# A sort's scatters held two block steps later behind TensorE in a graph network kernel

## The chip, the cores and the metric

One core of a Trainium2 chip runs the whole program in one launch. The metric is the device time of that core in microseconds, the median of several runs. The kernel before took 1187.74 us (three runs: 1185.68, 1187.74, 1198.05).

## The reference, cut to what matters

The input is a table `x` of 50,000 nodes by 128 features and 12,500 edges, each with a source node, a destination node and 40 attributes (3, 5 and 32 of them). With `h = relu(layernorm(x))` the result is `x` plus a graph layer of `h`:

```
h  = maximum(layernorm(x), 0)
xx = resmlp(h, weights 0)                 # every node: x + silu(silu(x) w1 + b1) w2 + b2, then silu, wout
xs, xp, xd = resmlp(h, weights 1..3)[dst] # gathered for each edge
s = xx + segment_sum(gs * xs, src)        # gs, gp, gd come from the 32 edge attributes
p = segment_sum(gp * xp, src);  d = segment_sum(gd * xd, src)   # gp also times pij (3), gd times dij (5)
y = s + (pa * pb).sum + (da * db).sum     # pa, pb = halves of p w_pp;  da, db = halves of d w_pd
out = x + resmlp(y, weights 4)
```

The segment sums need the edges ordered by source node, and the kernel sorts them itself.

## The kernel before, in words

**Stages.** The program has three stages: a node stage (about the first 410 us), an edge stage and a final stage. In the node stage the 50,000 rows are cut into 98 blocks of 512 rows (four tiles of 128). Each block is loaded, normalised (VectorE and ScalarE share it, lines 618 to 637 and 774 to 788), stored to a table `node_h`, transposed by TensorE (L871), sent through three matrix products (L884, L891, L899) with a ScalarE activation after each of the first three TensorE operations (L798, L808, L817), copied out (L823) and stored. TensorE does this for 94 blocks in a software pipeline: in step k it transposes block k, does the first product of block k-1, the second of block k-2 and the output product of block k-3. One such step is called a block step here, and its number is that of the block transposed.

**The sort beside it.** In the same stage a radix sort with two passes, one per digit of the source number, orders 98 tiles of 128 edges. For each pass VectorE makes one-hot rows of the digits (L664), TensorE counts them (L834), and VectorE makes starting ranks (L672, L674). Then, in 14 chunks of seven tiles, TensorE keeps running counts (L859) and VectorE picks each edge's rank out of them (L681) and writes the ranks of the chunk (L693). GpSimd then moves the edges: each tile is one indirect DMA that writes 128 rows of 42 words to a table in device memory (L506). The first pass writes to `edges_by_low`, which GpSimd loads back into SBUF (L544, three parts) when all 98 scatters have landed; the second pass starts from that (digits L648, one-hots L664, in step 49 of VectorE's program), and writes to `edges_by_src`.

**Order around the change.** Each engine's program is written out by hand. VectorE's and ScalarE's work for a block is tied to TensorE by counting semaphores; `chunk()` (L268) places chunk c of a pass in step `chunks + 5c//2`. The ranks of a chunk after the first are written one step later. The first pass has `chunks` = 5, the second 53. GpSimd has nothing of the block work, only the scatters. `scatter` (L501) waits for the ranks of its chunk, and before each of its seven tiles it calls `keep_pace` (L474), which waits for TensorE:

```
quarter = 4 * ps.scatters + 5 * t // 3
n = quarter // 4
```

The quarter modulo four says which event is waited for: transposes of block n-1, first product of block n-2, second product of block n-3, or output product of block n-4. All four events lie in TensorE's step n-1. So twelve scatters are let go in five block steps, and the wait before tile 97 is for step 44 in the first pass and step 92 in the second. The field `scatters` is read in `keep_pace` only.

**What follows the scatters.** After the first pass GpSimd waits for all scatters and issues the three loads of `pay`; VectorE's next instruction (L648) waits for the first of them, and TensorE counts the new one-hots at fixed places of steps 49 to 52. Blocks 50 to 55 are normalised by ScalarE alone. After the second pass SyncE, which has issued the block loads and stores before, waits for all scatters and loads the first edge groups (`load_group`, L57 to L68); GpSimd waits for the first of these before it gathers rows (L74), and TensorE's first work of the edge stage (L1760) waits for the gathers.

Of the kernel before, what the change touches and what calls it, by code (L numbers as in the profile page):

```python
# [78 lines left out]
def gnn_kernel(nc, x, src, dst, attr3, attr32, attr5, w_rs, w_rp, w_rd, w_pp, w_pd,  # L79
# [54 lines left out]
    with ctx:  # L134
# [125 lines left out]
        class Pass:  # L260


            def __init__(self, n, made_at, counted_at, seeded_at, based_at, picked_at, chunks, alone, dram, width):
                self.n, self.made_at, self.counted_at, self.seeded_at = n, made_at, counted_at, seeded_at
                self.based_at, self.picked_at = based_at, picked_at
                self.chunks, self.scatters, self.alone, self.dram, self.width = chunks, chunks, alone, dram, width

            def chunk(self, k, lag=0):  # L268

# [1748 lines left out]
```

## Time and profile before

| what | value |
|---|---|
| median of three runs | 1187.74 us |
| the profiled execution | 1187.62 us, span 1185.8 us |
| TensorE busy | 1088.6 us, 92% |
| VectorE busy | 688.9 us, 58% |
| ScalarE busy | 736.6 us, 62% |
| GpSimd busy | 471.7 us, 40% |
| scatters of the first pass | 98, from 46.2 to 208.8 us |
| scatters of the second pass | 98, from 247.9 to 400.5 us |

Times in rows are from the start of the span. Outside the span lie 1.8 us of the profiled execution. In a timeline row the first number is the start and the second the duration, `x` the number of instructions merged, and the bracket gives the idle time of the engine before it and what ended it. The name "remote" or "another core or an unknown queue" stands where the releaser is not known to the profile.

### The profile page before, as it was taken

The page shows a single profiled execution, that of the slowest core. Times are in us where ns is not written, and L with a number is a line of the kernel's source. Part 1 is how long each engine was busy: PE and PEld are TensorE (multiplying, and loading weights), DVE is VectorE, ACT ScalarE, POOL GpSimd, SP SyncE. Part 2 cuts the span into 40 slices and gives each one's busy share as a digit, 9 for nine tenths or more (in the row PEclk, how much of TensorE's full clock was granted, in tenths as well). Part 3 has the DMA queues.
Part 4 walks back from the last instruction along what each step waited for, and adds up shares of the span by engine and source line. Part 5 has one row for each costly group of instructions (what it writes and reads, how often), then busy time and mean ns, then how long its engine had stood idle before and what let it go on. Part 6 is the DMA issues. An engine that isn't in the chain of part 4 may idle for free.

```text
span 1185.8 us, 22908 instructions
## 1 busy us (share of the span) xinstructions
PE 1088.6 (92%) x6267; PEld 711.7 (60%) x6267; DVE 688.9 (58%) x2413; ACT 736.6 (62%) x1379; POOL 471.7 (40%) x433
## 2 busy tenths in 40 slices
PE   4978998987898659999999999999979999999998
PEld 2645665765666326666666666666736666666665
DVE  8976776766666226656665665655633444444432
ACT  4656878966778635665565565555536666666664
POOL 2355666155666442556556656655440000000000
PEclk9988999999999879999999999999999999999999
DMA  9667767855674443665556555555549999999984
GB/s 267 208 201 232 225 223 222 296 170 175 224 228 155 142 94 75 115 118 107 97 102 107 99 95 106 101 96 92 101 69 240 282 268 274 274 271 273 269 275 142
DMA packets 319187, 210.81 MB, mean 178 GB/s; under 512 B 204084, under 2 KB 240830, under 8 KB 318963
## 3 DMA queue, kind: packets, MB, share of 16 engines
q1 hardware_dynamic: 280770, 164.67, 50.7%
q0 software_dynamic: 24208, 19.29, 10.3%
q10 hardware_dynamic: 14112, 25.70, 6.2%
q8 instruction: 44, 0.72, 0.3%
q14 instruction: 53, 0.43, 0.1%
HBM read 107.15 MB, written 102.42 MB: 177 GB/s over the span
## 4 chain that ended last, share of the span: by engine, by line
PE 83%; DVE 6%; issue 5%; ACT 2%; another core or an unknown queue 2%; DMA 2%; POOL 0%; SPq 0%; ACTq 0%; POOLq 0%; DVEq 0%
PE quad L1133 8%; PE bank L1147 7%; PE bank L1769 6%; PE quad L884 5%; PE quad L1139 5%; PE bank L1779 5%; PE bank L899 5%; PE bank L1845 4%; PE quad L891 4%; PE bank L1815 4%; PE bank L1846 3%; PE quad L871 3%; PE quad L1855 2%; PE quad L1122 2%
## 5 line engine op out<-in xcount | busy, mean ns | idle before, releaser
L1421 POOL DMA_INDIRECT node_sums<-rowout,row_i x98 | 154.8, 1580 | 49.6 <-issue 28.7
L74 POOL DMA_INDIRECT yin<-node_h,er x98 | 99.2, 1012 | 165.1 <-DMA nxt<-edges_by_src 130.9
L1054 DVE TENSOR_TENSOR rowout<-bank,xin 128x512 f32<-128x512 f32 x98 | 67.8, 692 | 142.7 <-PE bank L1147 141.7
L1147 PEld LDWEIGHTS bank<-wo_sb,s 128*128 128x128 f32 x784 | 102.8, 191 | 47.8 <-issue 47.8
L899 PEld LDWEIGHTS bank<-wo_sb,s 128*128 128x128 f32 x720 | 95.3, 194 | 54.6 <-issue 54.5
L506 POOL DMA_INDIRECT edges_by_low<-pay,rank_i x98 | 99.7, 1017 | 69.5 <-issue 28.9
L1473 DVE SCALAR_TENSOR_TENSOR h<-bank,b_sb,hT 128x512 f32<-128x512 f32 (+1 forms) x75 | 55.5, 740 | 123.3 <-PE bank L1779 113.6
L506 POOL DMA_INDIRECT edges_by_src<-pay,rank_i x98 | 98.9, 1009 | 60.8 <-issue 24.4
L784 ACT ACTIVATE xn<-xin,nbias,rnorm 128x128 f32<-128x128 f32 x222 | 106.4, 493 | 13.0 <-DVE nbias L616 10.5
L681 DVE SCALAR_TENSOR_TENSOR picked<-bank,onehot 128x256 bf16<-128x256 f32 (+1 forms) x196 | 67.5, 387 | 74.1 <-PE bank L859 29.6
L1133 PE MATMUL quad<-s,w_sb 128*128 128x512 f32 x196 | 103.8, 612 | 0.8 <-ACT s L1071 0.7
L1147 PE MATMUL bank<-wo_sb,s 128*128 128x128 f32 x784 | 103.5, 275 | 0.9 <-DVE rowout L1054 0.9
L899 PE MATMUL bank<-wo_sb,s 128*128 128x128 f32 x720 | 96.9, 278 | 7.9 <-ACT rowout L823 5.7
L884 PE MATMUL quad<-s,w_sb 128*128 128x512 f32 x188 | 101.8, 625 | 0.1
L565 DVE BATCH_NORM_STATS2 stat<-xin 128x6 f32<-128x128 f32 x392 | 98.6, 283 | 1.1 <-DMA xin<-in_x_dram 1.1
L1652 ACT ACTIVATE s<-h 128x512 f32<-128x512 f32 (+1 forms) x75 | 46.6, 622 | 72.7 <-DVE h L1473 56.6
L1681 ACT COPY AB<-bank 128x512 f32<-128x512 f32 x98 | 58.1, 593 | 54.1 <-PE bank L1846 41.9
L1769 PE MATMUL bank<-s,w_sb 128*128 128x512 f32 (+1 forms) x150 | 79.9, 615 | 6.9 <-ACT s L1644 4.8
L871 PE MATMUL quad<-ident,xn 128*128 128x128 f32 x284 | 45.5, 284 | 38.7 <-issue 21.0
L808 ACT ACTIVATE s<-quad,b_sb 128x512 f32<-128x512 f32 x94 | 64.6, 687 | 21.4 <-PE quad L884 11.9
L1779 PE MATMUL bank<-s,w_sb 128*128 128x512 f32 (+1 forms) x150 | 76.2, 590 | 0.1
L891 PE MATMUL quad<-s,w_sb 128*128 128x512 f32 x142 | 75.7, 616 | 0.0
(208 smaller groups left out, 2254.4 us busy)
## 6 DMA issues: line engine op xcount, KB each, us to landing
xin<-in_x_dram SPq DMA_DIRECT2D x196, 256.0 KB
node_h<-xn SPq DMA_DIRECT2D x98, 256.0 KB
out_dram<-rowout ACTq DMA_DIRECT2D x98, 256.0 KB
node_sums<-rowout SPq DMA_DIRECT2D x90, 256.0 KB
yin<-node_sums SPq DMA_DIRECT2D x53, 256.0 KB, 3.7
yin<-node_sums SPq DMA_DIRECT2D x180, 64.0 KB, 3.2
src_in_every_row<-edge_src_row SPq DMA_DIRECT2D x24, 256.0 KB
border_sums_by_tile<-border_sums SPq DMA_DIRECT2D x24, 256.0 KB, 2.1
```

Of the source, the lines that this page charges most:

```text
L74: pool.indirect_dma_start(out=xg[:, s, j, :], out_offset=None, in_=x, in_offset=bass.IndirectOffsetOnAxis(ap=er[:, s, j, 1:2].bitcast(mybi ...
L506: nc.gpsimd.indirect_dma_start(out=ps.dram, out_offset=bass.IndirectOffsetOnAxis(ap=rank_i[:, t:t + 1], axis=0), in_=pay[:, t, :], in_offs ...
L565: last = nc.vector.bn_stats(stat[:, b % 32, j, :], xin[:, s, j, :])
L784: ins = nc.scalar.activation(xn[:, b % 4, j, :], xin[:, s, j, :], ACT.Relu, bias=nbias[:, q, i:i + 1], scale=rnorm[:, q, i:i + 1])
L884: nc.tensor.matmul(BANK_A[:, :], w1_sb[:, m, :], s1[:, (k - 1) % 3, :], start=True, stop=True).then_inc(a_done, 1)
L891: nc.tensor.matmul(BANK_X[(k - 2) % 4][:, :], w2_sb[:, m, :], s2[:, (k - 2) % 3, :], start=False, stop=True, skip_group_check=True).then_i ...
L899: last = nc.tensor.matmul(BANK_O[:, j * P:(j + 1) * P], s3[:, (k - 3) % 3, j * P:(j + 1) * P], wo_sb[:, m, :], start=True, stop=True)
L1133: nc.tensor.matmul(BANK_A[:, :], w1_sb[:, m, :], s1[:, s, :], start=True, stop=True).then_inc(a_done, 1)
L1147: last = nc.tensor.matmul(BANK_O[:, j * P:(j + 1) * P], s3[:, s, j * P:(j + 1) * P], wo_sb[:, m, :], start=True, stop=True)
L1421: nc.gpsimd.indirect_dma_start(out=ysum, out_offset=bass.IndirectOffsetOnAxis(ap=row_i[:, t % 2, j:j + 1], axis=0), in_=urow[:, t % 2, j, ...
L1769: nc.tensor.matmul(BANK_A[:, 0:e], w1_sb[:, MLP[m], :], s1[:, k % 2, 0:e], start=True, stop=True).then_inc(a_done, 1)
L1779: nc.tensor.matmul(BANK_B[:, 0:e], w2_sb[:, MLP[m], :], s2[:, m, 0:e], start=True, stop=True).then_inc(b_done, 1)
```

## The change

Both passes get `scatters = chunks + 2` in place of `scatters = chunks`: 7 and 55 in place of 5 and 53. The quarter number of every scatter grows by eight, so that each of the 196 waits is for the same kind of event two block steps later. Tile 97 waits for step 46 in the first pass and for step 94 in the second (where the counts are capped at 94 and 90). No instruction is added or taken away.

```diff
@@ -263,7 +263,7 @@
             def __init__(self, n, made_at, counted_at, seeded_at, based_at, picked_at, chunks, alone, dram, width):
                 self.n, self.made_at, self.counted_at, self.seeded_at = n, made_at, counted_at, seeded_at
                 self.based_at, self.picked_at = based_at, picked_at
-                self.chunks, self.scatters, self.alone, self.dram, self.width = chunks, chunks, alone, dram, width
+                self.chunks, self.scatters, self.alone, self.dram, self.width = chunks, chunks + 2, alone, dram, width
 
             def chunk(self, k, lag=0):
```

## Rows read from the trace of the kernel before

**Rows 1.** The page, costliest groups: the scatters of the first pass.
```profile
L506 POOL DMA_INDIRECT edges_by_low<-pay,rank_i x98 | 99.7, 1017 | 69.5 <-issue 28.9
```

**Rows 2.** Windows, transposes L871 alone: stretch, length, PE, PEld, clock, DMA share, GB/s.
```profile
44.45:115.62 71.17, 9.70 (x56) 6.96 (x57) 0.86 0.69 223
115.62:205.50 89.88, 14.76 (x96) 10.55 (x97) 1.00 0.71 221
208.91:221.66 12.75, 2.46 (x16) 1.86 (x17) 1.00 0.89 307
260.61:301.80 41.19, 6.00 (x37) 4.28 (x37) 0.96 0.60 192
301.80:398.36 96.56, 16.07 (x104) 11.34 (x105) 1.00 0.59 195
```

**Rows 3.** Timeline of GpSimd, first and last scatter of one chunk.
```profile
58.91 0.96 POOL L506 DMA_INDIRECT edges_by_low<-pay,rank_i  x1 [3.96 <-DVE rank_i L693]
...
66.67 0.96 POOL L506 DMA_INDIRECT edges_by_low<-pay,rank_i  x1 [0.31 <-issue]
```

**Rows 4.** Timelines of TensorE and ScalarE beside that chunk, steps 10 and 11.
```profile
62.45 0.60 PE L871 MATMUL quad<-ident,xn 128*128 128x128 f32 x4
...
70.77 1.87 PE L884 MATMUL quad<-s,w_sb 128*128 128x512 f32 x2
...
67.59 0.60 ACT L798 ACTIVATE s<-quad 128x512 f32<-128x512 f32 x1 [3.73 <-remote]
```

**Rows 5.** The same timelines in the second pass, steps 61 and 91, and a scatter.
```profile
276.65 0.60 PE L871 MATMUL quad<-ident,xn 128*128 128x128 f32 x4
...
280.42 0.60 ACT L798 ACTIVATE s<-quad 128x512 f32<-128x512 f32 x1 [1.66 <-remote]
...
393.92 0.60 PE L871 MATMUL bank<-ident,xn 128*128 128x128 f32 x4
...
396.33 0.60 ACT L798 ACTIVATE s<-bank 128x512 f32<-128x512 f32 x1 [1.63 <-PE quad L884]
...
396.57 1.07 POOL L506 DMA_INDIRECT edges_by_src<-pay,rank_i  x1 [1.25 <-remote]
```

**Rows 6.** Timelines where the first pass ends: TensorE, GpSimd, VectorE, ScalarE.
```profile
205.97 1.02 PE L884 MATMUL quad<-s,w_sb 128*128 128x512 f32 x2
...
212.96 1.02 PE L884 MATMUL quad<-s,w_sb 128*128 128x512 f32 x2
...
239.82 2.52 PE L834 MATMUL bank<-onehot,ident_h 128*128 128x196 bf16 x28
...
208.77 1.14 POOL L506 DMA_INDIRECT edges_by_low<-pay,rank_i  x1 [0.30 <-issue]
212.12 1.67 POOL L544 DMA_DIRECT2D pay<-edges_by_low  x3 [2.21 <-DMA edges_by_low<-pay,rank_i]
...
217.88 0.18 DVE L648 CAST digit_i<-pay 128x28 int32<-128x28 f32 x1 [4.89 <-DMA pay<-edges_by_low]
...
229.94 7.66 DVE L664 TENSOR_SCALAR onehot<-digits_h,digit_f 128x196 bf16<-128x196 bf16 x42
...
242.45 0.36 DVE L749 CAST counts_h<-bank 128x196 bf16<-128x196 f32 x1 [2.52 <-PE bank L834]
...
252.29 0.49 ACT L784 ACTIVATE xn<-xin,nbias,rnorm 128x128 f32<-128x128 f32 x1 [1.34 <-DVE nbias L616]
```

**Rows 7.** Timelines where the second pass ends: GpSimd, TensorE, SyncE's queue.
```profile
400.53 1.16 POOL L506 DMA_INDIRECT edges_by_src<-pay,rank_i  x1 [0.30 <-issue]
412.97 0.99 POOL L74 DMA_INDIRECT yin<-node_h,er  x1 [11.27 <-DMA er<-edges_by_src]
...
401.44 0.60 PE L871 MATMUL quad<-ident,xn 128*128 128x128 f32 x4
...
403.82 1.10 PE L884 MATMUL quad<-s,w_sb 128*128 128x512 f32 x2
...
419.56 1.08 PE L1760 MATMUL quad<-ident,yin 128*128 128x128 f32 x4 [12.73 <-DMA yin<-node_h,er]
...
410.08 0.37 SPq L64 DMA_DIRECT2D er<-edges_by_src  x1
```

## The prediction

> **What bounds the kernel now.** The change moves 196 waits of one engine, so I read in this order: what the moved instruction costs, how fast the node stage goes with and without it, what happens in single steps, and then the two places where other work waits for the last scatter. The page's costliest groups show that a scatter takes 1017 ns of GpSimd [rows 1]. That engine is not the bound. TensorE's block step is, and the windows over the transposes give its length, as four transposes are one step [rows 2]. There are 14 steps in 71.17 us (5.08 us each) while the first pass's scatters start, then 24 steps in 89.88 us (3.745 us each). With no scatter running, the windows' third row has four steps in 12.75 us (3.19 us each). In the second pass there are 9 steps in 41.19 us (4.58 us each) and then 26 in 96.56 us (3.714 us each). So the stage is slow early in either pass, and fastest where GpSimd rests. DMA is no busier in the slow stretch than in the fast one, 0.69 and 0.71 [rows 2].
>
> The timelines say what differs. Early on, the scatters wait for ranks and not for TensorE. When a chunk's ranks come, all seven of its scatters go out back to back, and the row that opens such a run names the ranks as the releaser [rows 3]. The old pace allows it, because the wait before tile 7 is for an output product of step 6, while its ranks are written in VectorE's iteration 8. The gates move 7 x 5/12 = 2.92 steps per chunk and the ranks 2.5, so the ranks' lateness shrinks by 0.42 a chunk and is gone after about five. In those runs ScalarE gets its transposed block late. In step 10 the transposes start at 62.45 and ScalarE's activation of them at 67.59, which is 5.14 us later and just as the run of seven is over [rows 3, 4]. In step 61 it is 3.77 us. In a stretch where TensorE paces the scatters the long delay is 2.41 us, and the delay without trouble is under 1 us [rows 5]. I count six delays of the long kind, all beside runs of at least six scatters: three of 5.1 to 5.9 us in the first pass, three of 3.7 to 3.8 us in the second (a seventh, of 3.7 us, stands in a later, paced stretch). What holds the transposes' signal back is not in the trace, as the releaser is "remote". That it goes with unbroken runs is my reading.
>
> **The change part by part.** No instruction is added, and no other queue gains or loses a DMA. GpSimd's queue holds, behind the scatters, the three loads back, the corrections and the first gathers.
>
> *The pace early in each pass.* With eight quarters more, tile 7 waits for step 8 and tile 14 for step 11, about when their ranks are there. Ranks then no longer release seven at once, and each scatter has its own gate, 5/12 of a step apart: 1.56 us at 3.745 us a step, against 1.29 us from start to start inside a run (66.67 - 58.91 over six) [rows 2, 3]. I cost this as a gain. If the six long delays shrink to the paced 2.41 us, it is 3 x (5.14 - 2.41) + 3 x (3.77 - 2.41) = 8.2 + 4.1 = 12.3 us [rows 4, 5]. The ends are 0, if the delay comes from something else, and 26.5 us, if both slow stretches run at the later pace: 71.17 - 14 x 3.745 = 18.7 and 41.19 - 9 x 3.714 = 7.8 [rows 2]. The upper end has the clock in it too. Behind the long delay a pair of products takes 1.87 us in place of 1.02 [rows 4, 6], and the granted clock of that stretch is 0.86, between the two levels of 1.2 and 2.4 GHz [rows 2]. I take 12.3 because it rests on delays that I can point at.
>
> *The end of the first pass.* The last gate moves from the first product of step 44 to that of step 46, 212.96 - 205.97 = 6.99 us later [rows 6]. The last scatter, the load back and VectorE's first digit follow it, since each waits for the one before: 208.77, 212.12 and 217.88 become about 215.8, 219.1 and 224.9. VectorE already waited 4.89 us for this load, so all of the 6.99 us reaches the one-hots [rows 6]. TensorE has some air. Its last 28 counts start at 239.82 and take 2.52 us, so the last seven start near 241.7, and the last one-hot ends at 229.94 + 7.66 = 237.60. That is 4 us of air, so TensorE itself waits 3 us. VectorE has less. Behind the one-hots it does statistics, waits 2.52 us for the counts, and then makes ranks and norm constants for which ScalarE waits 1.34 us. That chain moves by 6.99 - 2.52 = 4.5 us and the next blocks with it [rows 6]. Ends: 3.0 and 7.0 us. I take 4.5, as ScalarE is seen waiting on this chain.
>
> *Two more steps with scatters.* Steps 45 and 46 ran with none, from 208.91, at 3.19 us on average; at the paced 3.745 us they cost 2 x 0.55 = 1.1 us [rows 2]. Steps 5 and 6, and 53, lose a few in turn, which I leave at nothing. Ends: 0 and 2 us.
>
> *The end of the second pass.* SyncE issues the first load of the edge stage at 410.08, long after the last scatter's start at 400.53, so it was waiting for its own stores and not for the scatters [rows 7]. The cover is thin. A scatter has landed about 2.21 us after its end [rows 6], so the old slack is 410.08 - (400.53 + 1.16 + 2.21) = 6.2 us. The new group of four starts at most 2.65 us behind the last transposes at 401.44 (396.57 - 393.92) and its last 3.96 us after its first, so at 408.05, and at the earliest at 404.92, when the product of step 94 is through. It lands between 408.3 and 411.4 [rows 5 to 7]. The load then moves by 0 to 1.3 us, and everything behind it (the gathers, TensorE's idle 12.73 us) moves with it. I take 0.7 us.
>
> *Sum.* -12.3 + 4.5 + 1.1 + 0.7 = -6.0 us. The profiled execution of before took 1187.62 us and the median is 1187.74, so either base gives 1181.6 us.
>
> **A rule against the gain.** The slow stretch moved 223 GB/s and the fast one 221, so traffic does not tell the two apart, and a run of scatters brings only a few more small writes into a step [rows 2]. The Trainium skill, "DMA: Bandwidth & Descriptors", section "Issuing engines are not separate DMA queues", says that DMAs of all issuing engines end on the same 16 DMA engines and interleave there. By that rule alone what counts is the work, which is unchanged, and the gain is nothing.
>
> **The rivals.**
> 1. *The runs were not the cause.* The same writes on the same engines cost the same wherever they stand, and only the late end is paid: 1187.6 + 4.5 + 1.1 + 0.7 = 1193.9 us. For it: "remote" names no engine, and delays of 2.41 us go on in paced stretches. Against it: the steps without scatters are the fastest of all [rows 2, 5].
> 2. *The whole early slowness was the runs.* The gain is 26.5 us, and 1187.6 - 26.5 + 6.3 = 1167.4 us. For it: paced steps reach 3.7 us right behind the slow ones. Against it: in the first slow stretch weights and zeros are moved too, and VectorE is still busy after the one-hots.
> 3. *Slower: the load back lands in a crowd.* It starts near 219.1, in a stretch with DMA at 0.89 and 307 GB/s [rows 2], and now shares it with the last scatters' writes. Every microsecond beyond the 6.99 goes into VectorE's wait. Before, it took 217.88 - 212.12 = 5.76 us. If it takes twice that and the gain fails too, the time is 1187.6 + (6.99 + 5.76 - 2.52) + 1.8 = 1199.6 us. It decides against the kernel once the load back lasts over 11 us. Before, it began in that same stretch and was not slow, which speaks against it.
> 4. *The waits don't bind.* If ranks were late throughout, nothing would move: 1187.7 us. The rows against it are those in which TensorE releases scatters to the end.
>
> **How the numbers follow.** The forecast gets 0.50, rival 1 gets 0.20, rival 2 gets 0.15, rival 3 gets 0.08 and rival 4 gets 0.07. The forecast's own range, with a gain of 6 to 18 us and costs of 4 to 9, is 1174 to 1191 us. To hold 8 in 10 the whole range reaches up to rival 1 with its upper costs, 1197, and down near rival 2, 1170. About 1% (11.9 us) is what a measurement of this kernel can tell from no change. Faster by over 1% is rival 2 and a fifth of the forecast: 0.15 + 0.09 = 0.24. Slower by over 1% is rival 3 and a little of rival 1: 0.09. Within 1%: 0.67.
>
> **What would show it.** In the new trace the scatters of chunks 1 to 4 should have gaps of TensorE's making, and the releases by ranks should be almost gone. No activation L798 should start over 3 us behind its transposes before step 20. The 14 steps from the seventh on should take some 60 to 65 us. The first digit (L648) should come about 7 us later against step 49's transposes, and VectorE's wait of 2.52 us for the counts should vanish. The first load of the edge stage should be within 1.5 us of its old distance from the last transposes. I am wrong if delays of 5 us stay although the runs are broken, if new runs of seven form under the new gates, or if the load back takes over 8 us.

## The result, and the profile after

The changed kernel takes 1171.02 us (median of four runs, 1169.22 to 1175.29). Beside it the kernel before took 1186.71 us (four runs, 1184.07 to 1198.05). The medians differ by 15.7 us, or 1.3%. The recorded ratio, which is not that of the medians, is 0.9853 with a 95% interval of 0.9816 to 0.989. So the kernel is faster here by 1.3 to 1.5%. The forecast was 1181.6 us, a gain of 6.0 us. Its sign was right and its size was not. On three other chips the same change makes the kernel 0.4 to 0.5% slower, as the experiments show, so the sign held only for a chip like this one. I call the chip of these two kernels the first chip. The record has no number for it and does not say outright that it is one and the same for both.

The profiled execution of after took 1172.58 us with a span of 1168.8 us, against 1185.8 us before. I laid the two spans side by side, cut at TensorE's transposes. These are windows over all engines of after: stretch, length, then busy time and count for PE, PEld, DVE, ACT and POOL, then the granted clock, DMA share and GB/s.

```profile
44.45:100.27 55.82, 50.12 (x261) 33.62 (x260) 51.33 (x300) 42.26 (x85) 33.40 (x33) 0.97 0.85 269
100.27:189.18 88.91, 82.19 (x442) 55.87 (x441) 66.64 (x358) 72.54 (x145) 58.94 (x58) 1.00 0.72 230
189.18:207.32 18.14, 15.85 (x82) 10.43 (x81) 4.56 (x21) 14.93 (x31) 9.22 (x11) 1.00 0.71 222
207.32:235.23 27.91, 24.76 (x184) 18.81 (x183) 25.04 (x132) 19.55 (x41) 3.28 (x4) 1.00 0.62 230
235.23:246.20 10.97, 10.20 (x58) 6.93 (x56) 10.63 (x64) 9.42 (x20) 6.47 (x7) 1.00 0.64 206
246.20:281.87 35.67, 31.52 (x174) 21.01 (x173) 25.19 (x140) 26.97 (x55) 21.33 (x23) 1.00 0.66 213
281.87:378.31 96.44, 87.84 (x472) 59.29 (x473) 61.13 (x328) 77.62 (x156) 61.41 (x62) 1.00 0.60 197
```

The same windows of before, for the stretches that changed most (the first, fourth, fifth and sixth):

```profile
44.45:115.62 71.17, 56.84 (x261) 37.33 (x260) 51.41 (x300) 43.44 (x85) 38.20 (x38) 0.86 0.69 223
...
221.66:246.02 24.36, 24.27 (x185) 18.93 (x184) 21.49 (x113) 19.19 (x41) 3.15 (x4) 1.00 0.63 230
246.02:260.61 14.59, 10.56 (x58) 6.85 (x56) 13.45 (x78) 9.57 (x21) 8.65 (x9) 1.00 0.49 157
260.61:301.80 41.19, 32.92 (x173) 22.07 (x173) 21.94 (x125) 27.31 (x55) 24.94 (x25) 0.96 0.60 192
```

The counts of matmuls agree, so each pair of windows holds the same work. A window's length less its PE busy time is TensorE's idle time, and that splits every difference into waiting and slower work:

| block steps | before | after | difference | of it TensorE idle | of it TensorE busy |
|---|---|---|---|---|---|
| 6 to 20 | 71.17 | 55.82 | -15.35 | -8.63 | -6.72 |
| 20 to 44 | 89.88 | 88.91 | -0.97 | -0.81 | -0.16 |
| 44 to 49 | 16.16 | 18.14 | +1.98 | +1.77 | +0.21 |
| 49 to 54, first pass's end | 24.36 | 27.91 | +3.55 | +3.06 | +0.49 |
| 54 to 57 | 14.59 | 10.97 | -3.62 | -3.26 | -0.36 |
| 57 to 66 | 41.19 | 35.67 | -5.52 | -4.12 | -1.40 |
| 66 to 92 | 96.56 | 96.44 | -0.12 | | |
| 92 to 93 | 3.08 | 3.38 | +0.30 | | |
| step 93 to the first edge load | 8.64 | 10.00 | +1.36 | | |
| the rest of the span | 775.7 | 777.1 | +1.4 | | |

That is -17.0 us in all. The gain is 25.5 us in four rows of the table and the losses are 8.6 us.

**The runs are broken up.** In the timeline of GpSimd in after, the scatters that answer to [rows 3] go out in threes, and TensorE opens each group. Not every later run is that short: the longest has eight scatters, from 148.5 to 159.5 us. In before the first of seven had waited for its ranks.

```profile
58.81 0.96 POOL L506 DMA_INDIRECT edges_by_low<-pay,rank_i  x1 [1.07 <-PE bank L899]
60.07 1.05 POOL L506 DMA_INDIRECT edges_by_low<-pay,rank_i  x1 [0.30 <-issue]
61.43 1.15 POOL L506 DMA_INDIRECT edges_by_low<-pay,rank_i  x1 [0.31 <-issue]
63.51 0.96 POOL L506 DMA_INDIRECT edges_by_low<-pay,rank_i  x1 [0.93 <-PE bank L899]
```

**The longest delays before step 20 are gone.** For [rows 4], step 10, the timelines of TensorE and ScalarE give the transposes at 61.67 and ScalarE's activation of them 2.08 us later (5.14 before). The longest such delay before step 20 is in step 17, 2.96 us:

```profile
61.67 0.63 PE L871 MATMUL quad<-ident,xn 128*128 128x128 f32 x4
...
87.59 0.60 PE L871 MATMUL quad<-ident,xn 128*128 128x128 f32 x4
...
63.75 0.60 ACT L798 ACTIVATE s<-quad 128x512 f32<-128x512 f32 x1
...
90.55 0.60 ACT L798 ACTIVATE s<-quad 128x512 f32<-128x512 f32 x1
```

The three longest of steps 6 to 19 were 5.14, 5.88 and 5.11 us and are 2.96, 2.59 and 2.58 us, which is 8.0 us less. TensorE's idle time there fell by 8.6 us. Its products also run at the higher level of the clock again: the granted clock of the stretch rose from 0.86 to 0.97 and PE busy fell by 6.7 us for the same 261 matmuls. Further on, two delays over 3 us remain, of 3.02 us in step 37 and 3.22 us in step 61.

**Other signals than the transposes' are late too.** In before, the timelines of TensorE and ScalarE show it twice. Near 84 us ScalarE waits 4.92 us for an output product that ended at 79.05, and TensorE then waits 3.78 us for ScalarE's copy of it. Near 256 us ScalarE starts on a second product (L891) and an output product (L899) 4.1 and 4.8 us after their ends, at 252.44 and 253.33:

```profile
84.47 0.58 ACT L823 COPY rowout<-bank 128x512 f32<-128x512 f32 x1 [4.92 <-remote]
85.20 1.19 PE L899 MATMUL bank<-wo_sb,s 128*128 128x128 f32 x4 [3.78 <-ACT rowout L823]
...
251.42 1.02 PE L891 MATMUL quad<-s,w_sb 128*128 128x512 f32 x2
252.28 1.05 PE L899 MATMUL bank<-wo_sb,s 128*128 128x128 f32 x8
...
256.54 0.69 ACT L817 ACTIVATE s<-quad,b_sb 128x512 f32<-128x512 f32 x1 [1.79 <-remote]
258.09 0.59 ACT L823 COPY rowout<-bank 128x512 f32<-128x512 f32 x1 [0.86 <-remote]
```

The trace also records when semaphores were raised, though no view prints it and some records are missing. Here each raise from 44 us to the last transposes that belongs to one instruction without doubt (about three quarters of TensorE's) is set against that instruction's end. The ends of matmuls are modelled.

| signals of | before: recorded | over 1 us late | latest | after: recorded | over 1 us late | latest |
|---|---|---|---|---|---|---|
| TensorE | 284 | 78 | 5.40 us | 293 | 65 | 2.73 us |
| VectorE | 392 | 1 | 1.31 us | 373 | 0 | 1.00 us |
| ScalarE | 222 | 0 | 0.01 us | 206 | 0 | 0.01 us |

The late ones belong to every kind of TensorE's work, and they arrive in bursts. In before L859, L884 and L891 end at 63.82, 64.68 and 65.54, and their signals are recorded at 69.07, 69.11 and 69.15. In steps 57 to 66 of before 11 recorded signals are over 1.8 us late, and two of them are of transposes; in after 3 are, and one of them is. The mean lateness of TensorE's signals fell from 1.24 to 0.53 us in steps 6 to 20 and from 1.38 to 0.58 us in steps 57 to 66. In steps 20 to 44, where the time hardly changed, it went from 0.54 to 0.63 us.

**The first pass's end is paid for.** The timelines of after answer to [rows 6], in the order of GpSimd, VectorE and TensorE:

```profile
200.67 0.96 POOL L506 DMA_INDIRECT edges_by_low<-pay,rank_i  x1 [0.30 <-issue]
204.00 1.67 POOL L544 DMA_DIRECT2D pay<-edges_by_low  x3 [2.37 <-DMA edges_by_low<-pay,rank_i]
...
209.73 0.18 DVE L648 CAST digit_i<-pay 128x28 int32<-128x28 f32 x1 [11.77 <-DMA pay<-edges_by_low]
...
231.69 0.34 DVE L749 CAST counts_h<-bank 128x196 bf16<-128x196 f32 x1
...
207.32 0.60 PE L871 MATMUL quad<-ident,xn 128*128 128x128 f32 x4
211.79 0.76 PE L834 MATMUL bank<-onehot,ident_h 128*128 128x196 bf16 x7 [1.25 <-DVE onehot L664]
...
229.49 0.76 PE L834 MATMUL bank<-onehot,ident_h 128*128 128x196 bf16 x7 [0.50 <-DVE onehot L664]
...
232.09 0.26 PE L840 MATMUL bank<-counts_h,ones_h 128*128 128x196 bf16 x1 [1.40 <-DVE counts_h L749]
```

L648 stood 3.78 us ahead of step 49's transposes before (217.88 and 221.66) and stands 2.41 us behind them now, 6.2 us later. VectorE's wait of 2.52 us for the counts has vanished, and TensorE waits 1.25 + 0.50 + 1.40 = 3.15 us instead. The load back took 209.73 - 204.00 = 5.73 us, against 5.76 before.

**The second pass's end**, for [rows 7], from the timelines of GpSimd, SyncE's queue and TensorE:

```profile
388.47 0.96 POOL L506 DMA_INDIRECT edges_by_src<-pay,rank_i  x1 [0.30 <-issue]
394.60 0.99 POOL L74 DMA_INDIRECT yin<-node_h,er  x1 [5.17 <-DMA er<-edges_by_src]
...
385.62 5.78 SPq L410 DMA_DIRECT2D node_h<-xn  x4
391.69 0.37 SPq L64 DMA_DIRECT2D er<-edges_by_src  x1
...
401.20 1.09 PE L1760 MATMUL quad<-ident,yin 128*128 128x128 f32 x4 [12.85 <-DMA yin<-node_h,er]
```

GpSimd waits 5.17 us for the edge load in place of 11.27. SyncE issues that load 0.29 us after its last node store has been issued (385.62 + 5.78), and 2.26 us after the last scatter's end, about the 2.21 us in which a scatter landed in [rows 6]. Both are near enough to be the one that bound it. Against step 93's transposes the last scatter starts 7.7 us later than before (from 0.9 us ahead of them to 6.8 us behind), and the load goes out 1.4 us later. So 6.3 us of the shift were hidden.

### The profile page after: what moved, and what is told of

Its sections match the earlier page's. It is cut to its first block, busy times and chain, and to the rows that moved or that the text cites. A ratio compares the mean times of both kernels' runs of the same rounds, so it can differ in the third digit from the quotient of the medians.

```text
span 1168.8 us, 22908 instructions
## 1 busy us (share of the span) xinstructions
PE 1082.8 (93%) x6267; PEld 707.0 (60%) x6267; DVE 689.3 (59%) x2413; ACT 736.0 (63%) x1379; POOL 468.9 (40%) x433
## 4 chain that ended last, share of the span: by engine, by line
PE 81%; DVE 6%; issue 6%; ACT 2%; DMA 2%; another core or an unknown queue 1%; POOL 1%; SPq 0%; ACTq 0%; POOLq 0%; DVEq 0%
PE quad L1133 8%; PE bank L1147 8%; PE bank L1769 6%; PE quad L1139 5%; PE bank L1779 5%; PE quad L884 5%; PE bank L899 5%; PE bank L1845 4%; PE bank L1815 4%; PE quad L891 4%; PE bank L1846 4%; PE quad L871 2%; PE quad L1122 2%; PE quad L1854 2%; PE quad L1855 2%
## 5 line engine op out<-in xcount | busy, mean ns | idle before, releaser
L899 PEld LDWEIGHTS bank<-wo_sb,s 128*128 128x128 f32 x720 | 93.3, 191 | 50.6 <-issue 49.9
L784 ACT ACTIVATE xn<-xin,nbias,rnorm 128x128 f32<-128x128 f32 x222 | 106.5, 493 | 12.4 <-DVE nbias L616 10.5
L1133 PE MATMUL quad<-s,w_sb 128*128 128x512 f32 x196 | 103.7, 611 | 0.8 <-ACT s L1071 0.7
L899 PE MATMUL bank<-wo_sb,s 128*128 128x128 f32 x720 | 95.9, 276 | 4.3 <-ACT rowout L823 2.3
L884 PE MATMUL quad<-s,w_sb 128*128 128x512 f32 x188 | 98.2, 604 | 1.3 <-ACT s L808 1.3
L1139 PE MATMUL quad<-s,w_sb 128*128 128x512 f32 x148 | 75.6, 592 | 0.0
L808 ACT ACTIVATE s<-quad,b_sb 128x512 f32<-128x512 f32 x94 | 64.6, 687 | 15.1 <-PE quad L884 13.3
L1079 ACT ACTIVATE s<-quad,b_sb 128x512 f32<-128x512 f32 x98 | 66.5, 679 | 11.2 <-PE quad L1133 11.1
```

The lines of the kernel that those rows point to most:

```text
L784: ins = nc.scalar.activation(xn[:, b % 4, j, :], xin[:, s, j, :], ACT.Relu, bias=nbias[:, q, i:i + 1], scale=rnorm[:, q, i:i + 1])
L884: nc.tensor.matmul(BANK_A[:, :], w1_sb[:, m, :], s1[:, (k - 1) % 3, :], start=True, stop=True).then_inc(a_done, 1)
L899: last = nc.tensor.matmul(BANK_O[:, j * P:(j + 1) * P], s3[:, (k - 3) % 3, j * P:(j + 1) * P], wo_sb[:, m, :], start=True, stop=True)
L1133: nc.tensor.matmul(BANK_A[:, :], w1_sb[:, m, :], s1[:, s, :], start=True, stop=True).then_inc(a_done, 1)
L1139: nc.tensor.matmul(BANK_X[s][:, :], w2_sb[:, m, :], s2[:, s, :], start=in_squares(k, 2), stop=True, skip_group_check=True).then_inc(b_done, 1)
```

## The experiments

Two theories stood against each other.

- **A.** The change gains because it takes away the late signals from TensorE to ScalarE, and costs what the ends cost.
- **B.** The unbroken runs of scatters do the harm by themselves, wherever the kernel runs, or the later scatters gain in some other way.

The four sets of experiments ran on four other chips (numbered 2, 10, 11 and 9 in the record), and there the kernel before takes 1116 to 1117 us, 70 us less than on the first. I compare every kernel only with the kernel before on its own chip.

### Set 1: each pass alone, a stretched pace, and gaps

First pass alone:

```diff
-self.scatters = chunks
+self.scatters = chunks + (2 if n == 0 else 0)
```

> Only the first pass is moved by two steps. Theory (unbroken runs of six or more scatters hold back TensorE's signals; broken by the later gates they don't): steps 6 to 20 take 56 us as after the change, in place of 71.2; the first pass's end costs some 5 us; the second pass keeps its long delays of 3.7 us. About 1187 - 15.3 - 1 + 2 + 3.5 = 1176 us. Rival (the gain comes from where the two trains stand to each other or to the other work of the whole stage, not from runs): no such split, with steps 6 to 20 over 65 us or a sum of the two halves far from 16 us.

Second pass alone, `chunks + (2 if n == 1 else 0)`:

> Only the second pass is moved. Theory: steps 6 to 20 take 71 us as before, the first pass ends as before, steps 54 to 66 lose about 9 us, the end of the stage costs 1.4 us: about 1187 - 9 + 1.4 = 1179 us. Rival (whole stage): no gain without the first pass's shift, 1187 us.

Both passes start two steps later and end at the old steps:

```diff
-self.scatters = chunks
+self.scatters = chunks + 2
...
-quarter = 4 * ps.scatters + 5 * t // 3
+quarter = 4 * ps.scatters + 153 * t // 97
```

> Gates start two steps later as in the change, but run closer together (153 quarters over 97 tiles), so that the last gate of either pass is where it was before, steps 44 and 92. Theory: the runs are broken all the same, so the gain of about 25 us stays (15.3 + 1 + 3.6 + 5.5), and the costs of the late ends (5.5 at the first, 1.4 at the second) go: 1162 to 1166 us. Rival (the whole train must stand two steps later): half the gain at most, 1175 to 1182 us.

Gaps on GpSimd in the kernel before, a memset of 1.3 us behind the third and sixth scatter of the first five chunks of either pass:

```diff
+if t < 35 and t % 7 in (2, 5):
+    if pads[0]:
+        pool.wait_ge(s_pad, pads[0])
+    pads[0] += 1
+    nc.gpsimd.memset(st32[:, REST:T, :], 0.0).then_inc(s_pad, 1)
```

> Gates as before the change; in chunks 0 to 4 of either pass a 1.27 us memset stands on GpSimd behind the third and the sixth scatter of the seven, so no run is longer than three. Theory: delays over 3 us behind the transposes go, steps 6 to 20 take 56 to 60 us, neither pass ends later: 1164 to 1172 us. Rival (the position of the scatters in the steps, by the gates, makes the gain): 1186 to 1190 us. Second rival (any busy GpSimd delays the others): no gain either.

Measured against 1116.92 us (22 runs) for the kernel before:

| kernel | median, us | ratio, 95% |
|---|---|---|
| first pass alone | 1121.62 | 1.0039 (1.0022 to 1.0056) |
| second pass alone | 1116.41 | 1.0007 (0.9994 to 1.002) |
| start later, end the same | 1115.92 | 0.999 (0.9981 to 1.0) |
| gaps | 1130.4 | 1.0117 (1.01 to 1.0134) |

None gained. The times expected for this set were those of a chip with late signals, and so none of them could be tried. The change's price stood alone: 4.7 us of the first pass and nothing of the second. The gaps made the kernel slower. They delay GpSimd's train, and most of their price lies where other work waits for it: against the kernel before of sets 2 and 4, steps 6 to 20 take 2.9 us more (51.92), steps 49 to 54 take 5.8 us more and the rest from step 93 on 5.3 us more, with the edge load 15.4 us behind step 93's transposes in place of 8.6. This experiment can't speak on the late signals, because here there are none, as the next set shows.

### Set 2: before and after, unaltered

> The kernel before, unchanged, profiled beside the next one. If this chip delays the transposes' signal as in the first trace, steps 6 to 20 take some 71 us and the kernel 1187 us. If not (as in the four runs so far, where the kernel before took 1117 us), steps 6 to 20 take about 51 us, GpSimd issues over 80 scatters back to back in each pass with no activation L798 more than 1.2 us behind its transposes, and the kernel takes 1117 us.

> The changed kernel, timed against the kernel before on one chip. If the chip shows the delays: some 16 us faster. If it does not: theory 1 (the gain was only the shortened delays, and what is left is the cost of the late end of the first pass) gives 4.5 to 5 us slower, about 1122 us. Theory 2 (a gain that needs no delays) gives faster by 10 us or more on this chip too.

Before took 1116.15 us (10 runs) and after 1120.21 us (7 runs), a ratio of 1.0042 (1.0029 to 1.0056). So the change itself is 4 us slower here. It was timed on two more chips in sets 3 and 4. Set 4 gave the trace that I read closest. First its windows over all engines, of the kernel before, for steps 6 to 20 and 57 to 66:

```profile
44.42:93.48 49.06, 46.70 (x262) 32.73 (x260) 48.47 (x287) 42.62 (x85) 34.63 (x35) 1.00 0.92 307
223.26:253.14 29.88, 29.88 (x175) 21.23 (x174) 24.74 (x137) 27.56 (x55) 22.43 (x23) 1.00 0.84 262
```

The first stretch takes 49.06 us where the first chip took 71.17, with the same matmuls and 2.36 us of idle time in place of 14.33. Then the timelines of TensorE, ScalarE and GpSimd for step 10 and its chunk of scatters, which answer to [rows 3, 4]:

```profile
59.95 0.60 PE L871 MATMUL quad<-ident,xn 128*128 128x128 f32 x4
...
60.64 0.60 ACT L798 ACTIVATE s<-quad 128x512 f32<-128x512 f32 x1
...
57.33 0.95 POOL L506 DMA_INDIRECT edges_by_low<-pay,rank_i  x1 [2.18 <-DVE rank_i L693]
58.59 1.14 POOL L506 DMA_INDIRECT edges_by_low<-pay,rank_i  x1 [0.31 <-PE quad L884]
60.03 0.96 POOL L506 DMA_INDIRECT edges_by_low<-pay,rank_i  x1 [0.31 <-issue]
```

The run of seven is there, opened by its ranks as on the first chip, and the activation starts 0.69 us after the transposes begin. From 67.2 to 154.3 us 67 scatters go out without a gap, and in the second pass 91 do, from 224.0 to 343.3. Over all 94 steps the longest delay is 1.15 us (1.13 and less outside step 1). So unbroken runs of scatters don't delay ScalarE by themselves. With the change slower on each of the three chips that ran it, the later scatters don't gain in some other way there either, and theory B falls.

### Set 3: a third chip, and four steps

> The changed kernel once more, unaltered, for a chip on which TensorE's signals come late. Theory A (the gain is the going of the late signals, the price is the first pass's end): where the kernel before takes 1184 to 1190 us, 1170 us, and steps 6 to 20 in 55 to 57 us; where it takes 1116 us, 1120 us. Theory B (the change gains by itself, whatever the signals): under 1 of the kernel before on every chip.

> The first pass alone two steps closer. Theory A: where the kernel before takes 1184 to 1190 us, it keeps the gain of steps 6 to 44 (some 16 us) and pays the first pass's end (some 5 us), and doesn't have the second pass's 9 us: 1176 us. Where the kernel before takes 1116 us: 1121 us, all 4.7 us in steps 49 to 54. Theory B: as the changed kernel's ratio, 0.985, on either.

> Both passes' scatters start two steps later and end at the steps of the kernel before (a pace of 153/97 quarter steps a scatter instead of 5/3). Theory A: where signals come late, the gain of the changed kernel without its price at the first pass's end, 1171 less 4 to 5 = 1166 us, if breaking up the early runs is what counts; where they do not, 1116 us as before. Theory B (the distance at the end matters too): no better than the changed kernel.

With `chunks + 4` in both passes:

> Four steps instead of two, both passes. Theory A: the first pass's end costs by the gate, 3.05 us a step: two steps cost 4.7 us of 6.1, so four cost 4.7 + 6.1 = 10.8 us in steps 49 to 54; at the second pass's end two steps cost nothing that showed, and two more at most their 6.1 us. Where the kernel before takes 1116 us: 1127 to 1133 us. Where it takes 1187 us: 1175 to 1184 us. Theory B (the price is the end's own fixed chain, paid once): 1120 to 1122 us where the kernel before takes 1116.

Measured against 1116.54 us (20 runs):

| kernel | median, us | ratio, 95% |
|---|---|---|
| the change | 1121.41 | 1.0035 (1.002 to 1.005) |
| first pass alone | 1120.75 | 1.0037 (1.0024 to 1.0051) |
| start later, end the same | 1116.39 | 0.9994 (0.9984 to 1.0005) |
| four steps | 1132.23 | 1.0132 (1.0115 to 1.0149) |

The price grows with the steps and lies in two places. These are the windows of steps 49 to 54 over all engines, for the kernel before (set 4), then the first pass alone and then four steps (both set 3):

```profile
187.94:212.30 24.36, 24.27 (x185) 18.93 (x184) 24.00 (x127) 19.20 (x41) 3.29 (x4) 1.00 0.66 242
```

```profile
188.21:217.98 29.77, 26.11 (x184) 19.62 (x183) 25.03 (x132) 19.69 (x41) 3.28 (x4) 0.94 0.60 211
```

```profile
187.94:224.31 36.37, 27.27 (x184) 20.67 (x183) 25.15 (x132) 19.59 (x41) 5.89 (x9) 0.86 0.51 176
```

Two steps cost 5.4 us in this trace and four cost 12.0, a little over two more block steps of 3.05 us for the second two. The timeline of TensorE with four steps shows the wait at the first one-hots:

```profile
200.17 1.32 PE L834 MATMUL bank<-onehot,ident_h 128*128 128x196 bf16 x7 [9.02 <-DVE onehot L664]
```

After an idle time of 9.02 us the same seven counts take 1.32 us in place of 0.76, so the wait costs once more in the clock (0.86 in this stretch). Theory A's 10.8 us left out this part. At the second pass's end, two steps cost nothing that shows, and four push the edge load from 8.6 to 14.0 us behind step 93's transposes. The timelines of GpSimd and SyncE's queue with four steps name the reason:

```profile
363.98 0.96 POOL L506 DMA_INDIRECT edges_by_src<-pay,rank_i  x1 [0.31 <-issue]
...
366.31 0.37 SPq L64 DMA_DIRECT2D er<-edges_by_src  x1
```

The load now goes out 1.37 us after the last scatter has ended. That end is bound by the scatters. With two steps the load keeps its place (8.7 us behind the transposes in all three traces).

### Set 4: a fourth chip, and more small writes

> The changed kernel unaltered on whichever chip this is. Theory A (the gain is the going of late signals; the price is the first pass's end): 4 to 5 us over the kernel before where that takes 1116 us, 14 to 18 us under it where it takes 1184 to 1190 us. Theory B (the change gains by itself): under the kernel before in both.

> The kernel before, unaltered, for its trace on this chip. Theory A: if it takes 1116 us, no transposes wait over 1.2 us for ScalarE and steps 6 to 20 take 49 to 51 us; if it takes 1184 to 1190 us, delays of 2.4 to 5 us beside unbroken runs of scatters, and 65 to 71 us.

One candidate for the late signals was left that I could make here: many small writes beside the scatters.

```diff
+if 7 <= k < 21:
+    for i in (2 * k - 14, 2 * k - 13):
+        sp.dma_start(spare_rows[i * P:(i + 1) * P, :], zeros[:, 0:64]).then_inc(s_spare, 16)
```

In the kernel before:

> The kernel before with two more writes of 128 rows of 256 bytes from a zeroed tile to DRAM in each of SP's block turns 7 to 20 (28 writes, about as many small packets again as the scatters make there). Theory A (many small writes are what makes TensorE's signals late): transposes wait 2 us and more for ScalarE in steps 7 to 20, and these steps take 55 us or more. Theory B (not the packets, but something that this chip does not have): these delays stay under 1.2 us, steps 6 to 20 take 49 to 54 us, and the time is 0 to 5 us over the kernel before.

In the changed kernel:

> The changed kernel with the same 28 small writes. Theory A: less is lost to late signals than without the change, so it is level with or under the run without it. Theory B: the same 4 us over the run without the change as without the writes.

Measured against 1116.71 us (13 runs): the change 1122.96 us, ratio 1.0049 (1.0032 to 1.0066). Before with the writes took 1116.92 us, 1.0005 (0.9993 to 1.0018), and after with the writes 1121.61 us, 1.0046 (1.0029 to 1.0063). With the writes, step 6 to 20 of the kernel before read as follows in the windows of the transposes (length, PE, PEld, clock, DMA share, GB/s):

```profile
44.77:93.81 49.04, 8.45 (x56) 6.54 (x57) 1.00 0.92 278
```

That is 49.04 us against 49.06 without them, and between steps 7 and 20 no activation starts over 0.69 us behind its transposes. So more small packets alone bring no delays on this chip. What they would do on the first chip is not tested, and these writes went out from SyncE's queue, not from GpSimd's. For the changed kernel the expectation was a choice between no loss and the same 4 us. It took 1121.61 us with the writes and 1122.96 without, and the runs of the two overlap, so the writes cost nothing that shows. The change costs 4.7 us with them and 6.3 without.

### The traces in one table

Lengths in us, from transposes to transposes, and from step 93 to the end of the span. The first two rows are the first chip.

| kernel | 6 to 20 | 20 to 49 | 49 to 54 | 54 to 93 | 93 to end |
|---|---|---|---|---|---|
| before, first chip | 71.17 | 106.04 | 24.36 | 155.42 | 784.4 |
| after, first chip | 55.82 | 107.05 | 27.91 | 146.46 | 787.1 |
| before, sets 2 and 4 | 49.05, 49.06 | 94.46, 94.46 | 24.44, 24.36 | 128.02, 128.01 | 772.5, 772.6 |
| after, sets 2, 3, 4 | 49.04, 50.72, 50.73 | 94.47 in each | 28.80, 28.62, 27.54 | 128.07, 128.07, 128.08 | 771.4, 773.3, 774.6 |
| first pass alone, sets 1, 3 | 50.58, 49.04 | 94.46, 94.47 | 29.03, 29.77 | 128.01, 128.02 | 773.0, 772.7 |
| second pass alone | 50.72 | 94.47 | 24.35 | 128.07 | 771.4 |
| start later, end the same | 49.04, 49.05 | 94.47, 94.46 | 24.35, 24.35 | 128.02, 128.02 | 774.4, 773.5 |
| four steps | 49.04 | 94.47 | 36.37 | 128.00 | 777.9 |
| gaps | 51.92 | 94.72 | 30.16 | 128.02 | 777.9 |
| before with small writes | 49.05 | 94.47 | 24.35 | 128.01 | 773.7 |
| after with small writes | 50.74 | 94.47 | 29.62 | 128.07 | 771.4 |

The 1.7 us by which some first stretches are longer lie in one step (step 7 takes 5.55 us and not 3.86), where the granted clock is lower. They fall on the second pass alone too, whose first pass is that of the kernel before, and on the first chip before and after have the same 5.5 us in step 7. So they are no effect of the change. Leaving the gaps aside, what is left is one column: only steps 49 to 54 answer to a later first pass, by 3.2 to 5.4 us with two steps. The start-later kernel is level with before in both sets that have it (ratios 0.999 and 0.9994). It might keep most of the gain where signals come late, without the price, but no run of it fell on such a chip, so that is argued and not shown. On these chips its later gates don't break the second pass up: the scatters go out in runs of 7 and 91, as before.

In the fourteen traces of these four chips no recorded signal of TensorE comes more than 0.02 us after its matmul's end between 44 us and the last transposes (372 to 376 of them in each trace). The late signals are in the two traces of the first chip alone.

## Why the prediction was off, by its own steps

**The reading of the profile** held. The early slowness was in the steps where the six long delays were, and it went when the runs were broken. The delays before step 20 fell under 3 us (2.96 at most), the ranks no longer open runs of seven, and the first digit came 6.2 us later in place of about 7. The scatters don't go out singly, as the prediction had it, but mostly in threes to fives.

**The pace early in each pass, -12.3 us: the step that failed.** It measured -15.35 - 0.97 - 3.62 - 5.52 = -25.5 us. Of this 16.8 us are TensorE's idle time and 8.6 us its busy time. The term was the shrinking of six delays of the transposes' signal, and that came out nearly as priced: the three longest in steps 6 to 19 lost 8.0 us (8.2 foretold), and the three longest in steps 54 to 65 went from 3.76, 3.75 and 3.73 to 3.22, 2.63 and 2.38, which is 3.0 us (4.1 foretold). The failure is to let these 11 us stand for the whole. Two things were put at nothing. The first is the lateness of TensorE's other signals, the two products', the output product's and the counts', which fell too. No run splits the further 5.8 us of idle time, and these signals are the candidate for it: the wait of 3.78 us near 84 us is such a one, and it has gone (the longest wait of TensorE for that copy in these steps of after is 0.5 us). The second is the clock: PE busy fell by 8.6 us for the same matmuls, 6.7 of it in steps 6 to 20. I had [rows 2] for it (0.86) and named it as part of the upper end, but gave it nothing in the sum. The upper end of 26.5 us was worked out for steps 6 to 20 and 57 to 66 alone. Like for like these gave 20.9 us, and 4.6 us came from steps 20 to 44 and 54 to 57, where the bound had nothing. The steps' target of 60 to 65 us was missed on the good side, at 55.82.

**The first pass's end, +4.5 us.** It measured +3.55 on the first chip, 3.1 of it TensorE's idle time, and 3.2 to 5.4 us on the others, with a mean of 28.75 - 24.4 = 4.4 us over the five traces without gaps or writes. The place and the size were right. The chain was not quite the one I took: TensorE itself waits 3.15 us, near the 3 us foretold for it, while ScalarE's wait for norm constants (L784, now at 241.51) is 1.34 us as before, so nothing shows the part above 3 us that was put down to that chain. The sum did not have the clock that the wait costs (1.8 us of busy time in the trace with 3.7 us of idle time).

**Two more steps with scatters, +1.1 us.** Steps 44 to 49 grew by 1.98 us on the first chip. On the others, steps 20 to 49 take 94.46 or 94.47 us whatever the shift, so a scatter costs TensorE nothing that shows where signals are on time. The term is part of the same unknown as the delays.

**The second pass's end, +0.7 us.** The load went out 1.36 us further from the last transposes, just over the bound of 1.3, and 6.3 us were hidden where the prediction had a slack of 6.2. Elsewhere two steps are hidden, and the four-step kernel shows how much slack there was: its last scatter moves by 9.7 us against step 93's transposes (from 2.0 to 11.7 us behind them) and the load by 5.4, so 4.3 us were hidden.

**The rivals.** Rival 1, that only the late end is paid, is what the other chips show: 4.1, 4.9 and 6.3 us slower by the medians. The forecast's sign was right because the trace came from a chip with late signals, and that was luck: nothing in the prediction weighed the chip. Rival 2 (1167.4 us) is nearer to the first chip's 1171.02 than my forecast was. Rival 3 did not happen, as the load back took 5.73 us. Rival 4 falls with steps 6 to 20, which got 15.35 us shorter. The Trainium skill, "DMA: Bandwidth & Descriptors", section "Issuing engines are not separate DMA queues", states that DMAs of the scalar, sync and gpsimd engines run on the same 16 DMA engines and interleave. The prediction drew from it that a regrouping of the same scatters gains nothing. That conclusion agrees with the four other chips, where 87 us of unbroken scatters delay nobody, and not with the 15.7 us of the first.

**What stays open.** Why signals of TensorE come late on the first chip is not shown. That they come late, and that ScalarE's and all but one of VectorE's do not by over 1 us, is in its two traces. Whether the signal is held or the matmul itself ends late can't be told, as the ends are modelled. On that chip the longest delays went along with unbroken runs of scatters, and fell when most of these were broken. But a long run is not enough even there. Beside the run of seven at 46.2 us and that of six at 197.0 us of before, and the run of eight of after, L798 starts at most 1.8, 1.0 and 1.8 us behind its transposes (steps 6 to 8, 42 and 43, and 34 and 35). On four other chips the same runs, and longer ones, delay nobody, and on the one chip where more small packets were tried they don't either. The delays on the first chip are also not tied to scatters alone. At the start of its edge stage, beside twelve gathers issued back to back, the timelines of TensorE and VectorE have a transposed block used 4.6 us after it began:

```profile
425.77 0.28 PE L1890 MATMUL bank<-ident,border_keys 98*98 98x98 f32 x1
...
430.33 0.55 DVE L1556 TENSOR_SCALAR item_same<-bank,border_keys 98x98 f32<-98x98 f32 x2 [8.96 <-remote]
```

The kernel before on the fourth chip, the same two timelines:

```profile
364.53 0.40 PE L1890 MATMUL bank<-ident,border_keys 98*98 98x98 f32 x1
...
364.97 0.55 DVE L1556 TENSOR_SCALAR item_same<-bank,border_keys 98x98 f32<-98x98 f32 x2 [4.83 <-PE bank L1890]
```

There it takes 0.44 us. On the first chip the recorded signal of L1890 is 4.3 us late, and 4.0 us late in after too, so the change left this one as it was. What differs is the chip or its surroundings at the time, and the longest delays seen stand beside back-to-back indirect DMAs of GpSimd. Chip or surroundings, no run here can tell. Since no experiment fell on the first chip, that the breaking up of the runs (and not, say, the other block steps beside which the scatters now stand) took the delays away rests there on the comparison of two traces alone. Theory A's price is shown on four chips (on one of them with the first pass alone). Its gain is not shown on any but the first, by the result itself.

## What to carry to other kernels

Cost a stall with the clock that it takes down, on the gain's side and on the price's: here 15.35 us were 8.6 us of waiting and 6.7 us of slower products. And price a stage by the idle time of the engine that bounds it, not by the longest delays of one signal. When the releaser of a long wait is "remote", treat what goes along with it as a coincidence of this chip until another chip shows it too, and time the change on more than one. A gate on a chain with a deadline is best moved at its slack end only: on two chips starting later and ending at the old step cost nothing that shows, while ending two steps later cost 3 to 5 us.

## What the runs showed of the hardware

- The same kernel takes 1187 us on one chip and 1116 to 1117 us on four others, with instructions of the same length (a scatter of the first pass 1017 ns on the first and on the fourth chip, ScalarE's L784 493 and 491 ns). Of the 72.9 us between these two traces 61.1 are gone by the last transposes of the node stage (401.44 and 340.31), all of it in steps 6 to 49 and 54 to 93, in which GpSimd has scatters: steps 49 to 54 take 24.36 us on both.
- On the first chip 31 of 94 activations L798 start over 1.2 us behind their transposes before the change, and 39 after it. On the fourth chip none does. The change made the longest delays shorter, and it did not make delays fewer.
- The late signals of the first chip are TensorE's, whatever the instruction: 78 of 284 recorded ones over 1 us after the matmul's end in before (at most 5.40 us), beside none of 222 of ScalarE and 1 of 392 of VectorE. The late ones arrive in bursts, some 0.04 us apart (69.07, 69.11, 69.15). On the other four chips all of TensorE's recorded ones come within 0.02 us.
- On the fourth chip GpSimd issues 91 scatters of 128 rows on end from 224.0 to 343.3 us, one every 1.31 us on average, and TensorE's steps beside them stay at 3.05 and 3.66 us.
